# Attention layer of a two-layer tower: where the query and key products stand among the transposes

## The chip, the cores and the metric

The kernel is one program on 1 NeuronCore of a Trainium2 chip. The metric is the device time of one launch in microseconds (us). TensorE (PE) does matmuls and transposes, VectorE (DVE) and ScalarE (ACT) elementwise work, GpSimd (POOL) some more of it; SyncE (SP) issues DMAs. The engines run their own instruction streams in order and meet through semaphores.

## The reference, cut to what matters

16 sequences of 129 tokens (one class token, 128 others), 512 wide, pass four sublayers. Each one is h = h + f(layernorm(h)). The third, the one of this case, is gated linear attention:

```
x = layernorm(h)                      # per token, over 512
q = silu(x @ Wq.T) * SCALE            # Wq, Wk: 32 x 512
k = sigmoid(x @ Wk.T)
g = log_sigmoid(-k)
S_t = exp(g_t) * S_{t-1} + k_t v_t^T  # v = x, state 32 x 512
o_t = q_t S_t
go = o @ Wog.T + x @ Wig.T
f = rms_norm(o) * g_weight * go * sigmoid(go)
```

A mixture-of-experts layer stands before it and another behind it.

## The kernel before, in words

Tokens lie in 17 tiles: tile 16 (`NB`) has the 16 class tokens, and tiles 0 to 15 have 128 tokens of one sequence each. `ORDER` takes tile 16 first, so position i = 0 is the class tile and position i is tile i - 1 for i = 1 to 16. The norm is solved in four groups (`GROUPS`): the class tile, positions 1 to 4, positions 5 to 10, and positions 11 to 16. For each group VectorE takes statistics (L482), aggregates them (L506), solves the inverse root by small dependent instructions (L516 to L522) and writes the normed tiles into `xn` one by one (L527).

**TensorE** (`tensor` of `gla_layer`) waits for each tile of `xn` and turns it by four 128 x 128 transposes (`turn_tile`, L538) into one of three PSUM banks (`TB1`), so turn i also waits until ScalarE has copied out turn i - 3 (`tev`). A *quarter* q is four tiles, positions 4q + 1 to 4q + 4. `project(q)` (L2001) multiplies the four turned tiles of a quarter, 512 tokens, by the 64 query and key columns, in 4 fp32 matmuls that the profile records as 8. It waits for the copies of all turns up to position 4q + 4, writes into its own bank (`QK_BANKS[q]`) and raises `qk`. `project(-1)` does the 16 class tokens. Before the change the projections 0, 1 and 2 stand behind the turns at positions 6, 10 and 14, and projection 3 behind all.

**ScalarE** (`scalar`) copies each turn out into `xg` (L1920; two quarters fit, so a copy of quarter 2 or 3 waits for projection 0 or 1). `band_cls` (L1926, L1927) handles the class tokens. `band_of(q)` waits for projection q and writes queries (L1932, a copy) and keys (L1933, a sigmoid) of that quarter into 32 partitions. Before the change `band_of(0)`, `(1)` and `(2)` stand behind the copies at positions 7, 11 and 15, and `band_of(3)` behind all. Then two sigmoids over all quarters follow (L1948, L1949), and the copies of a second pass of turns (L1955).

**Behind it** TensorE goes through the tiles a second time: it turns each again, multiplies by the split gate weights (`rows_by`, L2029), does the attention products (L2054, L2061) and the outputs (L2080 to L2087). VectorE runs the decay scan and scales the keys (L1784 to L1805) once the sigmoids are there. SyncE waits for all five projections (`qk` at 5) before it loads the next layer's first shared weights.

Of the kernel before, what the change touches and what calls it, by code (L numbers as in the profile page):

```python
# [533 lines left out]
def turn_tile(t_eng, ps_bank, xn, t, ident):  # L534

    r = tile_rows(t)
    for k in range(KD):
        ins = t_eng.transpose(ps_bank[:, k * r:(k + 1) * r], xn[0:r, t, k * P:(k + 1) * P], ident[0:r, 0:r])  # L538
    return ins
# [1142 lines left out]
def gla_layer(nc, sem, sb, ps, d, hd, h_in, h_got, g, before, stored, xr_next, rest):  # L1682
# [7 lines left out]
    KH, BL, NBL, NG = 32, 32, 4, 4  # L1690
# [214 lines left out]
    def scalar(s):  # L1905
        s.wait_ge(w_in, 5 * 16)
        for w, to in ((wog, wo), (wig, wi)):
            s.activation(to[:, 0], w, ACT.Copy).then_inc(wsp, 1)

        def turn(i):  # L1910
            n = ORDER[i]
            r, q = rows_of(n), n // NG
            s.wait_ge(turned, i + 1)
            src = ps[:, TB1[i % 3], 0:KD * r].rearrange("p (k n) -> p k n", k=KD)
            if n == NB:
                s.activation(xg16, src, ACT.Copy).then_inc(tev, 1)
                return
            if q >= 2:
                s.wait_ge(qk, q)
            s.activation(xg[:, q % 2, :, (n % NG) * P:(n % NG + 1) * P], src, ACT.Copy).then_inc(tev, 1)  # L1920

        def band_cls():
            s.wait_ge(qk, 1)
            for q, band in enumerate(bands):
                cols = slice(NG * q, NG * q + NG)
                s.activation(qr[band, :, 0], ps[0:KH, CLS_BANK, cols], ACT.Copy).then_inc(bnd, 1)  # L1926
                s.activation(kk[band, :, 0], ps[KH:2 * KH, CLS_BANK, cols], ACT.Sigmoid).then_inc(bnd, 1)  # L1927

        def band_of(q):
            s.wait_ge(qk, q + 2)  # L1930
            src = ps[:, QK_BANKS[q], :].rearrange("p (b n) -> p b n", b=NG)
            s.activation(qr[bands[q], :, 1:SEQ], src[0:KH], ACT.Copy).then_inc(bnd, 1)  # L1932
            s.activation(kk[bands[q], :, 1:SEQ], src[KH:2 * KH], ACT.Sigmoid).then_inc(bnd, 1)  # L1933

        for i in range(T):
            turn(i)
            if i == 3:
                band_cls()
                for to in (xc3[0:NB], xc3[2 * KH:ROWS3]):
                    if to is not None:  # L1940
                        s.wait_ge(c3, 2)
                        s.activation(to, xn[0:NB, NB, :], ACT.Copy).then_inc(c3, 1)
            if i % 4 == 3 and i > 4:
                band_of((i - 7) // 4)
        for q in range(NG - 1, NG):
            band_of(q)
        s.wait_ge(bnd, 4 * NG)
        s.activation(sq, qr, ACT.Sigmoid).then_inc(bnd, 1)  # L1948
        s.activation(av, kk, ACT.Sigmoid, scale=-1.0).then_inc(bnd, 1)  # L1949

        def high_part(j):
            n = ORDER[j]
            r = rows_of(n)
            s.wait_ge(turned, T + j + 1)
            s.activation(xT[:, j % 2, 0, :, 0:r], ps[:, TB2[j % 2], 0:KD * r].rearrange("p (k n) -> p k n", k=KD), ACT.Copy).then_inc(tev, 1)  # L1955

        def xw_out(j):
            n = ORDER[j]
            r = rows_of(n)
            s.wait_ge(xwp, j + 1)  # L1960
            if j == 0:
                s.activation(xwc3[0:NB], ps[0:NB, XW_BANK, :], ACT.Copy).then_inc(c3, 1)
                s.activation(xwc3[2 * KH:ROWS3], ps[0:NB, XW_BANK, :], ACT.Copy).then_inc(c3, 1)
            s.activation(xw[0:r, j % 2], ps[0:r, XW_BANK, :], ACT.Copy).then_inc(xwr, 1)

        def square(j):
            r, u = rows_of(ORDER[j]), j % 2
            s.wait_ge(ob, j + 1)
            if j:
                s.wait_ge(ssr, j)  # L1970
            s.activation(junk[0:r], ps[0:r, O_BANKS[u], :], ACT.Square, accum_out=ss[0:r, j:j + 1]).then_inc(ssr, 1)

        def gate(j):
            r, u = rows_of(ORDER[j]), j % 2
            s.wait_ge(gor, j + 1)
            if j >= 2:
                s.wait_ge(pr, j - 1)
            s.activation(sg[0:r, u], ps[0:r, G_BANKS[u], :], ACT.Sigmoid).then_inc(sgr, 1)

        high_part(0)  # L1980
        high_part(1)
        xw_out(0)
        xw_out(1)
        s.wait_ge(acp, 1)
        s.activation(accF[0:ROWS3], ps[0:ROWS3, ACC_BANK, :], ACT.Copy).then_inc(atcr, 1)
        for j in range(T):
            if j >= 1 and j + 1 < T:
                high_part(j + 1)
            if 1 <= j and j + 1 < T:
                xw_out(j + 1)  # L1990
            square(j)
            gate(j)

    def tensor(t):
        t.wait_ge(w_in, 5 * 16)

        def project(q):
            w, bank = (NB, CLS_BANK) if q < 0 else (QC, QK_BANKS[q])
            t.wait_ge(tev, 1 if q < 0 else 4 * q + 5)
            for k in range(KD):  # L2000
                mm = t.matmul(ps[0:2 * KH, bank, 0:w], wqk[:, k, :], xg16[:, k, :] if q < 0 else xg[:, q % 2, k, :], start=(k == 0), stop=(k == KD - 1))  # L2001
            mm.then_inc(qk, 1)

        for i, n in enumerate(ORDER):
            t.wait_ge(xr, i + 1)
            if i >= 3:
                t.wait_ge(tev, i - 2)
            turn_tile(t, ps[:, TB1[i % 3], :], xn, n, ident).then_inc(turned, 1)
            if i == 3:
                project(-1)  # L2010
            if i % 4 == 2 and i > 4:
                project((i - 6) // 4)
        project(NG - 1)

        PARTS = ((0, 0), (0, 1), (1, 0))

# [81 lines left out]
        for j in range(T):  # L2098
# [8 lines left out]
            outs(j)  # L2107

    return sync, vector, gpsimd, scalar, tensor, qk


# [204 lines left out]
```

## Time and profile before

| | us |
|---|---|
| median of 3 runs | 1591.97 |
| lowest and highest | 1591.94, 1593.3 |
| the profiled execution, its time | 1593.97 |
| the profiled execution, its span | 1592.2 |
| TensorE busy with matmuls | 1389.7 |
| VectorE busy | 833.2 |
| ScalarE busy | 373.7 |
| mean granted clock of TensorE | 0.964 |

The span runs from the first instruction to the last. Busy time of an engine is a sum over stages with different limits, so it doesn't say what a change in one stage is worth. The granted clock is 1.0 at 2.4 GHz and 0.5 at 1.2 GHz, and a stretch with both shows a value between. The stage of this change lies between 661 and 707 us of the span.

### The profile page before, as it was taken

The numbers are of one execution on the slowest core, as the hardware profiler recorded it, in microseconds if no ns is written. First come the engines' busy times: TensorE is split into PE (matmuls) and PEld (weight loads), VectorE is DVE, ScalarE is ACT, GpSimd is POOL, SyncE is SP. The second block draws the span as 40 slices with busy tenths as digits, with TensorE's granted clock in tenths as the row PEclk, the third lists the DMA queues.
The fourth block names the chain that finished last, engine by engine and source line by source line (L and its number), as shares of the span: only waits on it lengthen the run. The fifth ranks groups of instructions, "written<-read, shape, count | busy, mean of one in ns | idle before, by whom it ended". The sixth has DMA issues, their size and how long they took to land.

```text
span 1592.2 us, 20911 instructions
## 1 busy us (share of the span) xinstructions
PE 1389.7 (87%) x6461; PEld 1077.6 (68%) x6462; DVE 833.2 (52%) x1711; ACT 373.7 (23%) x711; POOL 480.7 (30%) x350
## 2 busy tenths in 40 slices
PE   0585739999899999289999899999999979989996
PEld 0583317888444444137776688888888869879885
DVE  8875597655222222563667765555555533323332
ACT  1113114221111111232222312332333212212221
POOL 0662430351244443001211035433332111333441
PEclk9999779999999999689999999999999999999998
DMA  4492005102955554600000404666666588666553
GB/s 97 92 162 32 0 21 179 61 21 68 344 95 94 93 94 66 196 21 0 1 0 1 140 21 133 219 214 219 207 214 207 215 312 276 178 181 179 92 86 40
DMA packets 87387, 193.95 MB, mean 122 GB/s; under 512 B 28657, under 2 KB 32753, under 8 KB 83825
## 3 DMA queue, kind: packets, MB, share of 16 engines
q1 hardware_dynamic: 67232, 151.18, 29.4%
q0 software_dynamic: 20096, 42.02, 14.7%
q8 instruction: 33, 0.54, 0.1%
q14 instruction: 26, 0.21, 0.0%
HBM read 112.24 MB, written 77.87 MB: 119 GB/s over the span
## 4 chain that ended last, share of the span: by engine, by line
PE 62%; DMA 20%; DVE 11%; issue 4%; ACT 1%; POOL 0%; SPq 0%; POOLq 0%; DVEq 0%; ACTq 0%
PE ps L1507 22%; PE ps L1567 19%; DMA h_rows<-moe_scratch 7%; DMA h_rows<-held,moe_scratch 6%; PE ps L2029 6%; PE ps L429 4%; DMA out<-held,moe_scratch 3%; DVE held L482 2%; DMA out<-moe_scratch 2%; PE ps L538 1%; PE ps L2001 1%; PE ps L778 1%; PE ps L779 1%; PE ps L2054 1%; PE ps L1601 1%
## 5 line engine op out<-in xcount | busy, mean ns | idle before, releaser
L1567 PE MATMUL ps<-moe_rounded 128*128 128x384 f32 (+2 forms) x1800 | 374.1, 350 | 0.0
L1567 PEld LDWEIGHTS ps<-moe_rounded 128*128 128x128 f32 x1800 | 325.7, 188 | 32.9
L1277 DVE SCALAR_TENSOR_TENSOR held<-ps,moe_scratch,held 128x512 f32<-128x512 f32 (+1 forms) x255 | 187.4, 747 | 179.1 <-PE ps L1507 178.9
L1507 PE MATMUL ps<-moe_expert_parts,moe_rows_parts 128*128 (+1 forms) x1320 | 258.3, 348 | 4.7 <-DVE moe_rows_parts L1285 3.2
L1507 PE MATMUL ps<-moe_rounded 128*128 128x512 f32 (+3 forms) x885 | 239.2, 390 | 7.7 <-DVE moe_rounded L1259 5.7
L1507 PEld LDWEIGHTS ps<-moe_expert_parts,moe_rows_parts 128*128 128x128 f32 (+1 forms) x1320 | 218.7, 189 | 18.1 <-issue 5.4
L1507 PEld LDWEIGHTS ps<-moe_rounded 128*128 128x128 f32 (+2 forms) x885 | 145.4, 170 | 45.8 <-DVE moe_rounded L1259 8.1
L1291 DVE TENSOR_TENSOR moe_scratch<-moe_scratch,ps 128x256 f32<-128x256 f32 (+1 forms) x80 | 37.7, 471 | 230.2 <-ACT moe_scratch L1488 230.2
L1628 PE MATMUL ps<-moe_experts,moe_scratch 128*128 x320 | 145.9, 599 | 1.7 <-ACT moe_scratch L1474 1.1
L1383 POOL TENSOR_TENSOR moe_split_parts<-moe_scratch,moe_split_parts 128x704 fp32r<-128x704 f32 (+2 forms) x48 | 88.7, 1854 | 172.7 <-ACT moe_split_parts L1463 172.6
L1367 POOL DMA_INDIRECT slot_tokens<-moe_scratch x68 | 73.6, 1082 | 168.5 <-DVE held L1277 161.5
L1488 ACT ACTIVATE moe_scratch<-ps 128x256 f32<-128x256 f32 (+1 forms) x80 | 34.0, 425 | 326.8 <-PE ps L1628 191.5
L1450 ACT ACTIVATE moe_scratch<-ps 128x384 f32<-128x384 f32 (+2 forms) x75 | 38.7, 516 | 305.1 <-PE ps L1567 305.1
L429 PE MATMUL ps<-sb 128*128 128x64 f32 x256 | 56.5, 422 | 58.5 <-DVE sb L363 58.2
L2029 PE MATMUL ps<-gla_rounded 128*128 128x512 f32 (+1 forms) x408 | 100.8, 404 | 2.1 <-ACT gla_rounded L1955 2.1
L1628 PEld LDWEIGHTS ps<-moe_experts,moe_scratch 128*128 128x128 f32 x320 | 58.2, 192 | 60.7 <-issue 60.7
L429 PEld LDWEIGHTS ps<-sb 128*128 128x128 f32 x256 | 55.2, 332 | 59.3 <-POOL sb L384 57.9
L538 PE MATMUL ps<-held,moe_xn 128*128 128x128 f32 (+1 forms) x272 | 42.8, 306 | 59.5 <-DVE moe_xn L527 52.6
L2029 PEld LDWEIGHTS ps<-gla_rounded 128*128 128x128 f32 (+1 forms) x408 | 74.7, 186 | 22.4 <-issue 2.9
L538 PEld LDWEIGHTS ps<-held,moe_xn 128*128 128x128 f32 (+1 forms) x272 | 36.0, 160 | 74.5 <-DVE moe_xn L527 36.6
L1903 POOL TENSOR_TENSOR moe_xn<-moe_scratch 128x512 f32<-128x512 f32 (+1 forms) x17 | 25.6, 1506 | 199.2 <-DVE moe_scratch L1837 199.2
L1654 PE MATMUL ps<-moe_experts,moe_scratch 128*128 x160 | 75.4, 593 | 1.1 <-DVE moe_scratch L1313 1.1
(305 smaller groups left out, 1679.2 us busy)
## 6 DMA issues: line engine op xcount, KB each, us to landing
moe_expert_parts<-expert_parts SPq DMA_DIRECT2D x8, 3840.0 KB, 14.7
expert_parts<-moe_split_parts SPq DMA_DIRECT2D x32, 704.0 KB, 3.7
moe_scratch<-in_ffn_gate_up SPq DMA_DIRECT2D x32, 352.0 KB, 5.0
xn_rows<-moe_xn SPq DMA_DIRECT2D x2, 4096.0 KB, 12.8
moe_experts<-in_ffn_gate_up SPq DMA_DIRECT2D x8, 1024.0 KB, 12.6
expert_parts<-moe_split_parts SPq DMA_DIRECT2D x8, 1024.0 KB, 4.7
moe_scratch<-in_ffn_sh_gate_up SPq DMA_DIRECT2D x15, 512.0 KB, 3.5
tokens<-sb SPq DMA_DIRECT2D x16, 256.0 KB, 4.5
```

The source lines that it names most:

```text
L429: mm = t.matmul(o, ub[:, u, hh, :], bb[:, u, hh, :], start=True, stop=True)
L538: ins = t_eng.transpose(ps_bank[:, k * r:(k + 1) * r], xn[0:r, t, k * P:(k + 1) * P], ident[0:r, 0:r])
L1277: v.scalar_tensor_tensor(out=hb[0:rows, t, :], in0=ps[0:rows, ADDED[t % 3], :], scalar=sg[0:rows, t:t + 1], in1=hb[0:rows, t, :], op0=ALU. ...
L1291: v.tensor_tensor(ehid[:, u], esil[:, u], e_up(u), ALU.mult).then_inc(ehr, 1)
L1367: p.indirect_dma_start(out=slots, out_offset=bass.IndirectOffsetOnAxis(ap=pos_u[0:r, j, t:t + 1], axis=0), in_=tab_u[0:r, t, j, :], in_off ...
L1383: p.tensor_tensor(part[0:rows, x, 1, 0:w], raw[0:rows, x, 0:w], part[0:rows, x, 0, 0:w], ALU.subtract).then_inc(plr, 1)
L1450: s.activation(unit_sil(u, m), unit_banks(u, m)[0], ACT.Silu).then_inc(silr, 1)
L1507: mm = t.matmul(out, lhs(k, x), rhs(k, y), start=(k == 0 and i == 0), stop=(k == ks - 1 and i == 2))
L1567: mm = t.matmul(unit_banks(u, m)[j], weights(k, x, j), xT[y][:, k, unit_cols(m)], start=(k == 0 and i == 0), stop=(k == KD - 1 and i == 2))
L1628: mm = t.matmul(ps[:, u, 0:2 * F], xgT[:, u, k], exg(e, k, 0, 2 * F), start=(k == 0), stop=(k == KD - 1))
L1654: mm = t.matmul(ps[:, 6 + u, :], ehT[0:FR[f], u, f, :], exd(e, f, FR[f]), start=(f == 0), stop=(f == NF - 1))
L2029: mm = t.matmul(out[0:r], xT[:, j % 2, x, k, 0:r], w[:, y, k, :], start=(k == 0 and i == 0), stop=(stop and k == KD - 1 and i == 2))
```

## The change

Projection 0 moves from behind turn 6 to behind turn 4, which is the last turn of its norm group. Projection 1 stays behind turn 10, also the last of its group. Projection 2 moves from behind turn 14 to behind turn 16, right ahead of projection 3. On ScalarE `band_of(0)` moves from behind copy 7 to behind copy 8, `band_of(1)` from behind copy 11 to behind copy 12, and `band_of(2)` from behind copy 15 to behind copy 16, ahead of `band_of(3)`. No instruction is added or removed; the waits inside the moved functions move with them.

```diff
@@ ScalarE @@
-            if i % 4 == 3 and i > 4:
-                band_of((i - 7) // 4)
-        for q in range(NG - 1, NG):
+            if i == 8:
+                band_of(0)
+            if i == 12:
+                band_of(1)
+        for q in range(2, NG):
             band_of(q)
@@ TensorE @@
             if i == 3:
                 project(-1)
-            if i % 4 == 2 and i > 4:
-                project((i - 6) // 4)
-        project(NG - 1)
+            if i == 4:
+                project(0)
+            if i == 10:
+                project(1)
+        for q in range(2, NG):
+            project(q)
```

## Rows read from the trace of the kernel before

**Rows 1.** The page: span, then the chain that ended last, by engine and line.
```profile
span 1592.2 us, 20911 instructions
...
PE 62%; DMA 20%; DVE 11%; issue 4%; ACT 1%; POOL 0%; SPq 0%; POOLq 0%; DVEq 0%; ACTq 0%
```
**Rows 2.** Waits from 675 to 707: waiter, releaser, us in total, times, longest.
```profile
DVE gla_rounded L1774 <- ACT gla_rounded L1955: 14.1, 1, 14.1
...
ACT sb L1932 <- PE ps L2001: 5.4, 1, 5.4
...
PE ps L2001 <- ACT moe_scratch L1920: 4.2, 3, 2.1
```
**Rows 3.** Timeline of TensorE: start, length, what; in brackets idle before it, releaser.
```profile
670.86 1.12 PE L538 MATMUL ps<-held,moe_xn 128*128 128x128 f32 x4
675.63 1.97 PE L538 MATMUL ps<-held,moe_xn 128*128 128x128 f32 x8 [3.65 <-DVE moe_xn L527]
677.53 4.54 PE L2001 MATMUL ps<-moe_scratch,gla_raw 128*64 128x512 f32 x8
681.99 2.07 PE L538 MATMUL ps<-held,moe_xn 128*128 128x128 f32 x16
685.04 3.65 PE L2001 MATMUL ps<-moe_scratch,gla_raw 128*64 128x512 f32 x8 [0.98 <-ACT moe_scratch L1920]
688.62 2.07 PE L538 MATMUL ps<-held,moe_xn 128*128 128x128 f32 x16
691.81 3.65 PE L2001 MATMUL ps<-moe_scratch,gla_raw 128*64 128x512 f32 x8 [1.12 <-ACT moe_scratch L1920]
695.39 1.09 PE L538 MATMUL ps<-held,moe_xn 128*128 128x128 f32 x8
698.58 5.34 PE L2001 MATMUL ps<-moe_scratch,gla_raw 128*64 128x512 f32 x8 [2.09 <-ACT moe_scratch L1920]
...
706.94 9.42 PE L2029 MATMUL ps<-gla_rounded 128*16 128x512 f32 x33 [2.09 <-ACT gla_rounded L1955]
```
**Rows 4.** Timeline of ScalarE, the same columns.
```profile
675.09 0.60 ACT L1920 ACTIVATE moe_scratch<-ps 128x512 f32<-128x512 f32 x1
...
683.18 0.57 ACT L1932 ACTIVATE sb<-ps 32x512 f32<-32x512 f32 x1
683.78 0.59 ACT L1933 ACTIVATE sb<-ps 32x512 f32<-32x512 f32 x1
684.39 1.57 ACT L1920 ACTIVATE moe_scratch<-ps 128x512 f32<-128x512 f32 x3
...
696.71 0.58 ACT L1932 ACTIVATE sb<-ps 32x512 f32<-32x512 f32 x1
697.31 0.59 ACT L1933 ACTIVATE sb<-ps 32x512 f32<-32x512 f32 x1
697.92 0.60 ACT L1920 ACTIVATE moe_scratch<-ps 128x512 f32<-128x512 f32 x1
703.96 0.58 ACT L1932 ACTIVATE sb<-ps 32x512 f32<-32x512 f32 x1 [5.43 <-PE ps L2001]
```
**Rows 5.** Timeline of VectorE: the normed tiles of the last two groups, the same columns.
```profile
675.03 2.83 DVE L527 TENSOR_SCALAR moe_xn<-held 128x512 f32<-128x512 f32 x6
...
684.43 2.83 DVE L527 TENSOR_SCALAR moe_xn<-held 128x512 f32<-128x512 f32 x6
```
**Rows 6.** Stretches: length, busy of PE, PEld, DVE, ACT, POOL; granted clock, DMA share, GB/s.
```profile
675.70:679.60 3.90, 3.90 (x11) 2.19 (x12) 3.90 (x9) 1.20 (x2) 0.00 (x0) 0.53 0.01 2
...
683.50:700.10 16.60, 12.40 (x49) 5.49 (x49) 8.76 (x14) 8.13 (x15) 0.00 (x0) 0.99 0.01 1
700.20:703.50 3.30, 3.30 (x5) 0.69 (x4) 0.00 (x0) 0.00 (x0) 0.00 (x0) 0.54 0.00 0
703.60:706.90 3.30, 1.25 (x9) 0.74 (x8) 0.28 (x2) 2.87 (x6) 0.00 (x0) 0.96 0.59 184
...
724.10:730.80 6.70, 6.51 (x22) 5.23 (x21) 3.06 (x6) 0.89 (x2) 1.27 (x1) 0.52 0.00 0
730.90:870.60 139.70, 139.70 (x631) 104.86 (x630) 84.57 (x224) 37.42 (x80) 23.06 (x15) 1.00 0.00 1
```

## The prediction

> **What bounds the kernel now.** I read the page first. The span is 1592.2 us, and 62% of the chain that ended last is TensorE [rows 1]; the reader should see that the kernel has no spare engine to blame, but also that this says nothing of one stage. So next I read the waits of the stage in which the projections stand. TensorE's projections wait for ScalarE's copies of the turns, L1920, 3 times and 4.2 us in total; ScalarE waits 5.4 us for the last projection; and VectorE stands for 14.1 us until ScalarE's first copy of the second pass [rows 2]. That last wait is the important one: VectorE is not a competitor here, it idles until this stage is over, so whatever TensorE and ScalarE save here, it starts sooner.
>
> The timeline of TensorE shows where the 4.2 us lie: 0.98 ahead of projection 1, 1.12 ahead of projection 2, and 2.09 ahead of projection 3 [rows 3]. The timeline of ScalarE says why. Ahead of projection 3 the engine did not only copy turns 15 and 16: between them it did `band_of(2)`, 696.71 to 697.9, and only at 697.92 the copy of turn 16 that projection 3 waits for [rows 4]. In the same way `band_of(0)`, 683.18 to 684.37, stood ahead of the copy of turn 8, and projection 1 started at 685.04 right behind it [rows 3, 4]. VectorE had its part ready: the last six tiles were written from 684.43 to 687.26 [rows 5], while TensorE turned the first of them only at 688.62 [rows 3]. From turn 11 on the norm is no bound.
>
> Last I read the granted clock by stretches. It is at the lower level (1.2 GHz) until nearly 679.6, at the upper (2.4 GHz) from there to 700.1, at the lower from 700.2 to 703.5, and at the upper after it [rows 6]. The fall at 700 came 1.5 us into projection 3, after the 2.09 us gap. It shows in the duration: 5.34 us for the same 8 records that took 3.65 twice [rows 3]. So that gap cost 2.09 us as idle time and 5.34 - 3.65 = 1.69 us as a slow projection.
>
> **The change part by part.** No instruction comes or goes, so the sum is a new schedule of the same pieces. Prices at the upper clock: a projection 3.58 us from its start to the start of what follows (685.04 to 688.62), a turn 2.07 / 4 = 0.52 us, both [rows 3]; a copy 0.60 us alone and 1.57 / 3 = 0.52 us in a row, a band (both instructions) 684.39 - 683.18 = 1.21 us, both [rows 4].
>
> *Projection 0 behind turn 4.* It waits for copy 4, which runs from 675.09 to 675.69 [rows 4]. ScalarE can't make it sooner, since `band_cls` and two copies of the class tile stand ahead. Turns 5 and 6 are queued behind this wait and would have started at 675.63 [rows 3], when their first normed tile was written [rows 5]. So the added wait costs 0.1 us, and the 3.65 us in which TensorE stood idle before 675.63 are not filled: I give this "fill" nothing. If copy 4 came earlier by some other edit it would be worth up to that 3.65. Projection 0 now runs at the lower clock until 679.65: in those 3.95 us it gets half of that done, 1.98 of its 3.65, and ends at 681.3. The low stretch is spent either way, on two turns and half a projection before, on a projection after.
>
> *Turns 5 to 10 in a row.* 681.3 + 6 x 0.52 = 684.4. The three banks allow it: a turn needs the copy of three turns before, and copies at 0.52 to 0.60 us each keep up with turns at 0.52 with `band_of(0)` out of the way. It stands behind copy 8 now, at about 684.0. Projection 1 needs copy 8, ready at 684.0, so it starts at 684.4 without the wait of 0.98, and the next turns start at 688.0 instead of 688.62. Here the gain is only 0.6 us: 0.98 less what the later start of the turns at the low clock and the added wait took.
>
> *Turns 11 to 16 in a row.* Start 688.0. Copies 11 and 12 end at 689.1 and 689.7, `band_of(1)` runs to 690.9, copy 13 to 691.5. Turn 16 reuses the bank of turn 13 and waits for that copy, where it would have started at 690.6: a new stall of 0.9 us. Its bounds are 0 and 1.2, a whole band. The turns end at 692.0.
>
> *Projections 2 and 3 back to back.* Projection 2 runs 692.0 to 695.6. It covers copies 14 to 16, done by 693.1, so the waits of 1.12 and 2.09 both go. Projection 3 follows at once and ends at 699.2, if the clock holds. `band_of(2)` runs beside projection 3, 1.21 us under 3.6 us; without that cover it would come back on the path at its 1.21. Behind projection 3 all is as before: `band_of(3)` at once (0.03 us behind it in rows 4), two sigmoids, first copy of the second pass, and the next matmul 706.94 - 703.92 = 3.0 us behind the end of projection 3 [rows 3].
>
> *The sum.* Projection 3 ended at 703.92 and ends at 699.2: 4.7 us less. By kinds: waits of 4.2 go, 0.9 comes, 0.1 and about 0.2 of copies that trail are lost: 3.0 us of order; and 1.7 us of clock. Behind it nothing swallows the gain: TensorE is busy for all 139.7 us from 730.9 to 870.6 [rows 6], VectorE's 14.1 us wait only gets shorter with it, and SyncE's loads for the next layer wait for the same projections, so they move along. The profiled execution took 1593.97, so 1589.3. That execution was 2.0 us above the median of the runs, 1591.97, and the forecast goes by the median: 1587.3.
>
> *What I can only bound.* The clock's falls further on (0.52 over the 6.7 us from 724.1 [rows 6]) come at moments that I can't place for a program shifted by 4.7 us. One such fall is worth 1.7 us, by the 1.69 above. I take none, with 1.7 up and down as its bounds.
>
> **The rivals.** *The clock gives nothing.* Either the timed runs did not have the fall at 700 (the profiled execution is 2.0 us slower than the median, which is the size of one fall), or a new fall replaces it, because the stretch from 688 to 692 holds turns and a stall of 0.9 and no projection. Then only the order counts: 3.0 us, 1589.0. For it: the fall came where the gap was longest. Against: turns and a gap of 1.12 between projections 1 and 2 did not bring it down (0.99 from 683.5 to 700.1 [rows 6]). The Trainium skill, "TensorE: Matmul & The Clock Gate", section "Part 4: PE-mode transpose", says that transposes do not count as busy in the way matmuls do for the full clock. By that rule six turns in a row are a poor stretch, projection 2 would run at the lower level, and the time would be this rival's; this trace has turns only mixed with projections, so it neither bears it out nor refutes it.
>
> *The clock gives twice.* The stretch of small class products ahead of 724 moves too, and the 6.7 us low stretch becomes one of half the length: 1.7 us more, 1585.6.
>
> *No change.* ScalarE is the bound of the tail, so removing the order's waits only moves them to `band_of(3)`. Against it: ScalarE waited 5.4 us for the last projection [rows 2]. 1592.0.
>
> *Slower.* The projections use 64 of the 128 columns. If projection 0, alone at the front, does not raise the clock as the mix of two turns and a projection did at 679.6, the whole piece up to the end of projection 3 runs at the lower level. From 679.65 on it holds 18.6 us of TensorE work, which becomes 37.2; the 0.9 stall vanishes in it: 17.7 more, less the gain of 4.7, so 1605. Each us of low clock costs half a us of progress, so it decides from 9.4 us of additional low stretch on. Against it: from 700.2 to 703.5 nothing but projection 3 ran, at 0.54, and the clock was back up (0.96) in the stretch behind [rows 6].
>
> **How the numbers follow.** Forecast 0.55; clock gives nothing 0.25; clock gives twice 0.12; no change 0.05; slower 0.03. The forecast's own range is 1586.3 to 1588.5: the new stall between 0 and 1.2. The range with the clock's cases, and 1.7 either way behind the stage, is 1585.0 to 1590.2. Within 0.2%, 3.2 us, is about what a measurement of this kernel can't tell from no change; the border is 1588.8. Of the second case some two thirds lie inside it, all of the fourth and a little of the first: 0.24. Slower 0.03, faster 0.73.
>
> **What would show it.** Right: in the changed profile's TensorE timeline six turns stand in a row twice, the wait of L2001 for L1920 is under 0.3 us in total, turn 16 waits about 0.9, and the two last projections take 7.2 us together. Projection 0 starts between 675.6 and 675.8 relative to the same start of the norms. The 14.1 us wait of VectorE shrinks to about 9.4. Wrong: a projection of over 4 us behind 690, or a stretch of clock 0.5 between 690 and 700, says that the clock's share failed; a wait of turns 8 to 10 for copies says that ScalarE can't keep up; an equal end of the last projection with a gain elsewhere says that I named the wrong cause.

## The result, and the profile after

| | before | changed |
|---|---|---|
| median us (runs) | 1592.46 (14) | 1589.32 (14) |
| lowest to highest | 1588.72 to 1595.16 | 1587.16 to 1592.84 |
| profiled span | 1592.2 | 1588.1 |

The ratio of the times is 0.9981, 95% interval 0.9973 to 0.9989: 3.0 us less, 1.8 to 4.3. Run once more, beside new runs of the kernel before, the changed kernel gave 0.9973 (0.9962 to 0.9983). The forecast of 1587.3 is 2.0 us too low. The stated range of 1585.0 to 1590.2 held the time, and the direction was right. Half a us of the 2.0 is the kernel before: its median over 14 runs is 1592.46, and the forecast stood on 1591.97 from three.

TensorE's timeline of the changed kernel, which answers to [rows 3] (start, length, what; in brackets the idle time and what ended it):

```profile
669.96 0.66 PE L538 MATMUL ps<-held,moe_xn 128*128 128x128 f32 x4
674.83 6.02 PE L2003 MATMUL ps<-moe_scratch,gla_raw 128*64 128x512 f32 x8 [4.22 <-ACT moe_scratch L1920]
680.78 3.04 PE L538 MATMUL ps<-held,moe_xn 128*128 128x128 f32 x24
683.75 3.65 PE L2003 MATMUL ps<-moe_scratch,gla_raw 128*64 128x512 f32 x8
687.33 2.55 PE L538 MATMUL ps<-held,moe_xn 128*128 128x128 f32 x20
691.10 0.63 PE L538 MATMUL ps<-held,moe_xn 128*128 128x128 f32 x4 [1.22 <-ACT moe_scratch L1920]
691.66 7.08 PE L2003 MATMUL ps<-moe_scratch,gla_raw 128*64 128x512 f32 x16
...
701.76 5.72 PE L2034 MATMUL ps<-gla_rounded 128*16 128x512 f32 x24 [2.09 <-ACT gla_rounded L1957]
```

The three waits of 0.98, 1.12 and 2.09 us are gone. Two are left: 4.22 ahead of projection 0, in the place of the 3.65 ahead of turn 5, and a new one of 1.22 ahead of turn 16 (691.10). The two last projections run as one piece of 7.08 us. ScalarE shows what turn 16 waited for (to be held against [rows 4]):

```profile
688.02 1.09 ACT L1920 ACTIVATE moe_scratch<-ps 128x512 f32<-128x512 f32 x2 [2.32 <-PE ps L538]
689.13 0.59 ACT L1932 ACTIVATE sb<-ps 32x512 f32<-32x512 f32 x1
689.75 0.59 ACT L1933 ACTIVATE sb<-ps 32x512 f32<-32x512 f32 x1
690.36 2.06 ACT L1920 ACTIVATE moe_scratch<-ps 128x512 f32<-128x512 f32 x4
```

Band 1 stands between copies 12 and 13, and turn 16 needs the bank that copy 13 empties. The waits of the same stretch, answering to [rows 2]:

```profile
DVE gla_rounded L1774 <- ACT gla_rounded L1957: 9.4, 1, 9.4
...
PE ps L2003 <- ACT moe_scratch L1920: 4.2, 1, 4.2
...
PE ps L538 <- ACT moe_scratch L1920: 1.2, 1, 1.2
```

VectorE's wait fell from 14.1 to 9.4, as forecast. The first of the two PE waits is the one ahead of projection 0. The stretches (columns as in [rows 6]):

```profile
666.60:669.90 3.30, 3.26 (x20) 2.94 (x20) 3.30 (x7) 1.60 (x3) 0.00 (x0) 0.58 0.78 236
670.10:673.30 3.20, 0.52 (x4) 0.28 (x3) 2.94 (x15) 3.00 (x10) 0.00 (x0) 0.92 0.01 2
673.50:680.10 6.60, 5.27 (x7) 1.57 (x8) 6.41 (x16) 1.23 (x3) 0.00 (x0) 0.53 0.00 1
680.30:700.90 20.60, 18.16 (x82) 8.96 (x80) 11.15 (x29) 11.74 (x22) 0.00 (x0) 1.00 0.06 19
```

No fall between 680 and 701. Here the clock rose once already at 669.4 and fell again in the idle time ahead of projection 0.

I measure the **stage** from the start of the four-tile statistics (L482, 661.22 before, 660.72 after) to the end of projection 3. It was 703.92 - 661.22 = 42.7 us and is 698.74 - 660.72 = 38.0: 4.7 less between these two traces. The span lost 4.1. The rest adds up like this: 0.5 comes from ahead of the stage; behind it 1.2 is gained up to the last turns of the second pass (two pieces of low clock before, one after); and 2.2 are lost from there to the end, where the changed kernel's trace has low stretches at 926 and at 1284, of which this trace of before has none. The change touches no instruction there. The one at 1284 is in three other traces of the kernel before too. The one at 926 is in both traces of the changed kernel and in none of the four of the kernel before, whose clock is 1.00 from 925 to 935. It costs about half its 3.3 us, 1.6 us (an estimate: the clock was at half). So the shifted program may well lose again behind the stage a part of what it gained in it. Why it falls there is not shown: TensorE's wait just ahead is 1.77 us long in the changed kernel and 1.74 in the kernel before. The stretch in the two traces of the changed kernel, and then in the kernel before:

```profile
926.00:929.30 3.30, 3.30 (x11) 2.81 (x11) 0.95 (x2) 0.50 (x1) 1.92 (x2) 0.57 0.02 6
```

```profile
926.70:930.20 3.50, 3.50 (x11) 3.10 (x11) 1.17 (x2) 0.49 (x1) 1.67 (x2) 0.53 0.16 59
```

```profile
926.00:935.00 9.00, 7.26 (x37) 6.35 (x36) 6.76 (x10) 1.37 (x3) 1.78 (x2) 1.00 0.27 88
```

### The profile page after: what moved, and what is told of

It reads as the page before. It is cut to its first block, busy times and chain, and to the rows that moved or that the text cites. A ratio compares the mean times of both kernels' runs of the same rounds, so it can differ in the third digit from the quotient of the medians.

```text
span 1588.1 us, 20911 instructions
## 1 busy us (share of the span) xinstructions
PE 1388.7 (87%) x6461; PEld 1078.0 (68%) x6462; DVE 833.4 (52%) x1711; ACT 373.0 (23%) x711; POOL 480.2 (30%) x350
## 3 DMA queue, kind: packets, MB, share of 16 engines
q0 software_dynamic: 20096, 42.02, 14.6%
## 4 chain that ended last, share of the span: by engine, by line
PE 61%; DMA 21%; DVE 11%; issue 4%; ACT 2%; POOL 0%; SPq 0%; POOLq 0%; DVEq 0%; ACTq 0%
PE ps L1507 21%; PE ps L1567 19%; DMA h_rows<-moe_scratch 7%; DMA h_rows<-held,moe_scratch 6%; PE ps L2034 6%; PE ps L429 4%; DMA out<-moe_scratch 3%; DMA out<-held,moe_scratch 3%; PE ps L538 2%; DVE held L482 1%; PE ps L778 1%; PE ps L2003 1%; PE ps L779 1%; PE ps L2059 1%; PE ps L1601 1%
## 5 line engine op out<-in xcount | busy, mean ns | idle before, releaser
L1450 ACT ACTIVATE moe_scratch<-ps 128x384 f32<-128x384 f32 (+2 forms) x75 | 38.7, 515 | 306.9 <-PE ps L1567 301.5
```

What stands on the lines that cost most here:

```text
L1450: s.activation(unit_sil(u, m), unit_banks(u, m)[0], ACT.Silu).then_inc(silr, 1)
```

## The experiments

All edits are to the kernel named in each; "idle" is TensorE's idle time in the stage between turn 4 and the end of projection 3. Ratios are to runs of the kernel before on the same chip. Stages and idle times are from one trace each, where no number is given; in the two kernels with fills a fill counts as busy. Two traces of one kernel may differ in the stage by the clock. Their idle times agree better, but the clock enters there too: where turn 4 runs at the upper clock (0.66 us) and not at the lower (1.12), TensorE arrives sooner and stands up to 0.7 us longer ahead of the next piece. It did so in both traces of the changed kernel and in two of the kernel before.

| kernel | idle us | stage us | ratio (95%) | less than before, us |
|---|---|---|---|---|
| before, 4 traces | 7.8 to 8.5 | 41.2 to 42.7 | 1 | |
| changed, 2 traces | 5.4, 5.4 | 38.0, 38.6 | 0.9981 (0.9973 to 0.9989); again 0.9973 (0.9962 to 0.9983) | 3.0; 4.3 |
| act_only | 4.4 | 38.7 | 0.9960 (0.9947 to 0.9973) | 6.4 |
| pe_only | 7.9 | 40.7 | 0.9992 (0.9981 to 1.0003) | 1.3 |
| late_bands | 3.8 | 36.5 | 0.9971 (0.9961 to 0.9981) | 4.6 |
| cls_late | 2.8 | 35.2 | 0.9956 (0.9944 to 0.9969) | 7.0 |
| both | 0.7 | 34.4 | 0.9944 (0.9931 to 0.9957) | 8.9 |
| scalar_best | 4.4 | 38.4 | 0.9977 (0.9965 to 0.9989) | 3.7 |
| after_warm | 3.6 | 36.1 | 0.9970 (0.9956 to 0.9984) | 4.8 |
| before_filled | 6.0 | 41.3 | 0.9994 (0.9986 to 1.0003) | 1.0 |

**1. ScalarE's order alone** (act_only). The kernel before, with the ScalarE half of the diff.

> Only ScalarE's order is changed (bands 0, 1, 2 behind copies 8, 12, 16); TensorE's order is that of before. Stage length, from the start of the four-tile statistics (L482) to the end of projection 3, was 42.7 us before and 38.0 after the change. Theory A (the band ahead of an awaited copy was the cost; TensorE's order is worth nothing): projection 1 at once behind turn 10, projection 2 behind turn 14, a wait of 0.7 ahead of projection 3, stage 37.5 us, so 0.5 us better than the full change; time 3 to 5 us under before. Theory B (what counts is that projections 2 and 3 stand together behind all turns): stage 41 us or more and under 1.5 us of gain.

TensorE's timeline of this run, from projection 1 on:

```profile
684.21 3.65 PE L2003 MATMUL ps<-moe_scratch,gla_raw 128*64 128x512 f32 x8
687.79 2.06 PE L538 MATMUL ps<-held,moe_xn 128*128 128x128 f32 x16
689.79 3.65 PE L2003 MATMUL ps<-moe_scratch,gla_raw 128*64 128x512 f32 x8
693.36 1.09 PE L538 MATMUL ps<-held,moe_xn 128*128 128x128 f32 x8
695.20 3.65 PE L2003 MATMUL ps<-moe_scratch,gla_raw 128*64 128x512 f32 x8 [0.74 <-ACT moe_scratch L1920]
```

Of the waits only 0.74 us is left, as expected, and that with the projections still behind turns 10 and 14. The stage is 38.7 and not 37.5, since projection 0 took 5.78 us here and 4.54 in the trace from which I had worked it out: the same 8 records, more of them at the low clock. So by the stage it is not the 0.5 us better than the whole change that I expected; the time is 6.4 us less, more than the 3 to 5 expected, with 4.3 inside its interval. Theory B fell: putting projections 2 and 3 together is not what gains.

**2. TensorE's order alone** (pe_only). The kernel before, with the TensorE half of the diff.

> Only TensorE's order is changed; ScalarE's bands stay behind copies 7, 11 and 15. Theory A: band 2 now waits for projection 2 and stands ahead of copy 16, so projection 3 starts about 1.8 us behind projection 2; stage 40.7 us (42.4 if the clock falls in projection 3), 2.0 us of gain or 0.3. Theory B: stage 38 to 39 us, nearly the whole gain of the change.

The timelines of this run, TensorE's and then ScalarE's:

```profile
683.81 3.65 PE L2001 MATMUL ps<-moe_scratch,gla_raw 128*64 128x512 f32 x8 [0.97 <-ACT moe_scratch L1920]
...
690.67 1.11 PE L538 MATMUL ps<-held,moe_xn 128*128 128x128 f32 x8 [1.22 <-ACT moe_scratch L1920]
691.71 3.65 PE L2001 MATMUL ps<-moe_scratch,gla_raw 128*64 128x512 f32 x8
697.27 3.65 PE L2001 MATMUL ps<-moe_scratch,gla_raw 128*64 128x512 f32 x8 [1.91 <-ACT moe_scratch L1920]
```

```profile
695.40 0.58 ACT L1932 ACTIVATE sb<-ps 32x512 f32<-32x512 f32 x1 [3.41 <-PE ps L2001]
696.01 0.59 ACT L1933 ACTIVATE sb<-ps 32x512 f32<-32x512 f32 x1
696.62 0.60 ACT L1920 ACTIVATE moe_scratch<-ps 128x512 f32<-128x512 f32 x1
```

Stage 40.7 as worked out, and idle time of 7.9, the same as before: the waits moved and their sum stayed. The time can't be told from before. The stage is 0.4 us under the shortest of the four traces of before, so a small gain isn't excluded. ScalarE stood 3.41 us for projection 2 with copy 16 queued behind its band.

**3. Bands where they delay no copy** (late_bands).

```diff
-            if i == 8:
+            if i == 10:
                 band_of(0)
-            if i == 12:
+            if i == T - 1:
                 band_of(1)
```

> The changed kernel with band 0 behind copy 10 and band 1 behind copy 16, so that no band stands ahead of a copy that a turn waits for. Theory A: the stall of turn 16 (1.2 us in the changed kernel's trace) goes, stage 37.0 us against 38.0; 1 us less than the changed kernel. Rival (bands only move, ScalarE's sum is the bound of the tail): band 1 and band 2 delay band 3 and the stage's sigmoids, no gain.

TensorE's timeline from turn 11 on, and ScalarE's `band_of(3)`:

```profile
687.67 3.04 PE L538 MATMUL ps<-held,moe_xn 128*128 128x128 f32 x24
690.65 7.08 PE L2003 MATMUL ps<-moe_scratch,gla_raw 128*64 128x512 f32 x16
```

```profile
697.76 0.58 ACT L1932 ACTIVATE sb<-ps 32x512 f32<-32x512 f32 x1 [2.24 <-PE ps L2003]
```

Six turns in a row without a stall; stage 36.5. Against the changed kernel's 38.0 that is 1.5 less: 1.35 by the stall of turn 16, and 0.55 by the clock in projection 0 (5.47 against 6.02 us), which started 0.4 later. Bands 1 and 2 ran beside the projections and delayed nothing: band 3 found ScalarE idle for 2.24 us and started right behind projection 3, so the rival fell by the trace. The ratios, 4.6 us less against 3.0 and 4.3, overlap in their intervals and show no gain over the changed kernel.

**4. The idle time ahead of projection 0** (cls_late).

```diff
-            if i == 3:
+            if i == 4:
                 band_cls()
```

> The changed kernel with the class bands and the class copies behind copy 4 instead of copy 3, so that projection 0 can start at about 10 us from the start of the four-tile statistics instead of 14. Theory A (TensorE's 4.2 us of idle time ahead of projection 0 are only an order of ScalarE, and the path runs through projection 0): stage 34.6 us, 3.4 less than the changed kernel, and 6 to 8 us under before. Rival (the path runs through VectorE's last group of normed tiles, so an earlier projection 0 only waits for turn 11 instead): the gain stops at 0.6 to 1.5 us.

TensorE's timeline, from projection 0 on:

```profile
673.72 5.00 PE L2003 MATMUL ps<-moe_scratch,gla_raw 128*64 128x512 f32 x8 [0.69 <-ACT moe_scratch L1920]
...
686.11 2.55 PE L538 MATMUL ps<-held,moe_xn 128*128 128x128 f32 x20 [0.83 <-DVE moe_xn L527]
689.88 0.63 PE L538 MATMUL ps<-held,moe_xn 128*128 128x128 f32 x4 [1.23 <-ACT moe_scratch L1920]
```

Projection 0 starts 11.4 us into the stage instead of 14.1. The stage is 2.8 shorter than the changed kernel's (3.4 expected), and the time is 7.0 us less than before. Behind turn 4 VectorE now holds TensorE up for the first time, with 0.83 ahead of turn 11. The rival's bound of 0.6 to 1.5 was passed, so VectorE was not what bounded the changed kernel, but it is the next bound.

**5. Both of these** (both).

> The changed kernel with both of ScalarE's edits: class bands and copies behind copy 4, band 0 behind copy 10, band 1 behind copy 16. Theory A (each wait of TensorE for a copy is an order of ScalarE and they add): the stall of turn 16 (1.23 us in the run with the class copies late) goes and the idle time ahead of projection 0 stays at 0.7; what is left is 0.8 to 2.7 us of waiting for VectorE ahead of turn 11. Stage 34.0 us (35.24 with the class copies late alone, 36.52 with late bands alone), total 7 to 9 us under before. Rival (VectorE's last group sets the end, so the two don't add): stage 35 us, no better than the class copies late alone.

TensorE's timeline, from projection 0 to the end of projection 3, and VectorE's last six normed tiles:

```profile
672.55 6.40 PE L2003 MATMUL ps<-moe_scratch,gla_raw 128*64 128x512 f32 x8 [0.69 <-ACT moe_scratch L1920]
678.88 3.04 PE L538 MATMUL ps<-held,moe_xn 128*128 128x128 f32 x24
...
685.43 3.04 PE L538 MATMUL ps<-held,moe_xn 128*128 128x128 f32 x24
688.40 7.08 PE L2003 MATMUL ps<-moe_scratch,gla_raw 128*64 128x512 f32 x16
```

```profile
684.32 2.83 DVE L527 TENSOR_SCALAR moe_xn<-held 128x512 f32<-128x512 f32 x6
```

From 672.55 to 695.48 TensorE has no gap. The expected wait of 0.8 to 2.7 us ahead of turn 11 did not come, and that is luck of the clock: projection 0 took 6.40 us here and 5.00 in cls_late, so turn 11 came later than its tile, the first of the six from 684.32 on. Stage 34.4 (34.0 expected), median 1583.79 against 1592.29: the lowest time of this study, 8.9 us less than before (6.8 to 11.0). Its interval overlaps that of cls_late (4.9 to 8.9); that the two edits add is shown by the waits, not by the times.

**6. ScalarE's best order without TensorE's** (scalar_best). The kernel before with the class bands behind copy 4 and bands 0, 1, 2 behind copies 10, 14, 16.

> TensorE's order of before with all of ScalarE's edits: class bands and copies behind copy 4, band 0 behind copy 10, band 1 behind copy 14, band 2 behind copy 16. Theory A' (TensorE's early projection 0 is worth the idle time ahead of turn 5, but only once copy 4 is early): here TensorE still stands for 3.7 us ahead of turn 5, stage 37.4 to 38.7 us, 3 to 4 us longer than with both orders (34.37). Rival (TensorE's order is worth nothing, as ScalarE's order alone suggested): stage 34 to 35 us.

TensorE's timeline, turns 5 and 6, projection 0, and then projection 3:

```profile
675.74 1.97 PE L538 MATMUL ps<-held,moe_xn 128*128 128x128 f32 x8 [3.65 <-DVE moe_xn L527]
677.64 5.49 PE L2005 MATMUL ps<-moe_scratch,gla_raw 128*64 128x512 f32 x8
...
696.04 3.65 PE L2005 MATMUL ps<-moe_scratch,gla_raw 128*64 128x512 f32 x8 [0.74 <-ACT moe_scratch L1920]
```

Stage 38.4, 4.0 longer than with both orders, and the 3.65 us ahead of turn 5 stand as before. So TensorE's order shows no gain in the change as made, and is worth about 4 us of the stage once copy 4 is early: some 3.0 by the early projection 0 (3.65 us idle against 0.69), and 0.74 by the wait ahead of projection 3, which is gone where projection 2 stands there. The rival fell.

**7. What the low clock costs** (after_warm). The changed kernel; the added results are never read.

```diff
+        def fill(n):
+            for _ in range(n):
+                t.matmul(ps[0:2 * KH, QK_BANKS[3], :], wqk[:, 0, :], wog[:, 0, :], start=True, stop=True)
...
+            if i == 0:
+                fill(3)
...
             if i == 4:
+                fill(2)
                 project(0)
```

> The changed kernel with five 512-column matmuls whose result is never read, put into TensorE's idle times: three behind the class turn, two behind turn 4. Clock theory (the low clock from the start of the stage until about 680 costs what it lasts, since projection 0 is on the path): the clock is up before projection 0, which takes 3.65 us instead of 6.02, and the stage is 36.0 us against 38.0; time about 2 us under the changed kernel. Rival (projection 0 is not on the path, or low clock there is hidden by VectorE): stage stays at 38, time equal or up by the delay of turn 1.

The stretches of this kernel, then its projection 0:

```profile
662.30:667.50 5.20, 5.20 (x7) 1.14 (x6) 4.72 (x21) 0.22 (x1) 0.00 (x0) 0.50 1.05 388
667.60:670.00 2.40, 2.40 (x25) 2.20 (x24) 2.40 (x6) 1.74 (x5) 0.00 (x0) 1.00 0.82 255
670.20:674.40 4.20, 1.90 (x5) 0.43 (x4) 3.89 (x18) 3.97 (x11) 0.00 (x0) 1.00 0.09 22
```

```profile
674.46 5.29 PE L2003 MATMUL ps<-moe_scratch,gla_raw 128*64 128x512 f32 x8 [2.36 <-ACT moe_scratch L1920]
```

The stage came to 36.1, as expected, but only in part by the expected way. With the fill the clock was up from 667.6 on, yet it fell again at the start of projection 0, behind an idle piece of 2.36 us; projection 0 took 5.29, not 3.65. The other part is that faster turns let copy 4 and so projection 0 start earlier: 12.9 us into the stage instead of 14.1, 1.2 of the 1.9 us gained. In the time nothing of it can be seen: 1589.29 against 1588.37 for the changed kernel on the same chip.

**8. The fall ahead of projection 3** (before_filled). The kernel before, with `fill(2)` of experiment 7 ahead of `project(NG - 1)`.

> The kernel before with two 512-column matmuls whose result is never read ahead of the wait of projection 3, in the idle time of 2.09 us. Clock theory (the gap of 2.09 brings the clock down in projection 3, here and in a good part of the timed runs): projection 3 takes 3.65 us instead of 5.34, stage 41.0 instead of 42.7, time 0.8 to 1.7 us under before. Rival (the fall was chance of that execution, not tied to the gap): same time as before within 0.5 us. If the two matmuls don't fit they cost up to 0.3 us.

TensorE's timeline, the fill and projection 3:

```profile
697.58 1.93 PE L2006 MATMUL ps<-gla_raw 128*64 128x512 f32 x4
699.74 3.65 PE L2001 MATMUL ps<-moe_scratch,gla_raw 128*64 128x512 f32 x8 [0.23 <-ACT moe_scratch L1920]
```

Projection 3 took 3.65 us. The time is 0.9994 (0.9986 to 1.0003): it can't be told from before, and doesn't say how often there is a fall to prevent.

**9. Three more traces of the kernel before** (before_look1 to 3), unchanged.

> The kernel before once more, for its trace. If the fall of the clock in projection 3 belongs to the gap of 2.09 us, projection 3 takes 5.3 us here too; if it depends on how the chip's looks fall on the program, it takes 3.65 in some of the three traces and the forecast's term of 1.7 us was one execution's. Idle times 3.7, 1.0, 1.1 and 2.1 us in each.

> The same as for the first look at the kernel before: projection 3 of 5.3 us in all three by the first theory, of 3.65 in some by the second; stage 42.7 or 41.0 us accordingly.

> The same as for the first look at the kernel before. With the first trace that makes four: a share of about one half slow would put the clock's term of the forecast at 0.9 us on average instead of 1.7.

Projection 3 in each of the three:

```profile
697.02 3.65 PE L2001 MATMUL ps<-moe_scratch,gla_raw 128*64 128x512 f32 x8 [2.09 <-ACT moe_scratch L1920]
```

```profile
698.12 3.65 PE L2001 MATMUL ps<-moe_scratch,gla_raw 128*64 128x512 f32 x8 [2.09 <-ACT moe_scratch L1920]
```

```profile
699.48 3.65 PE L2001 MATMUL ps<-moe_scratch,gla_raw 128*64 128x512 f32 x8 [2.09 <-ACT moe_scratch L1920]
```

The wait is 2.09 us in all three. The slow projection is in none. The 5.34 us on which the forecast's clock term rests belong to one of four executions looked at. The idle time ahead of turn 5 was 4.32, 3.65 and 4.16 us, and not 3.7 in each: in the first and the third the clock was up for turn 4.

**Also run**: the changed kernel again (after_again).

> The changed kernel once more, for comparison on the same chip and for a second trace. Order theory: idle time of TensorE inside the stage 5.4 us again (4.2 and 1.2) and gain over before of 3 us. If the clock's share is real but not constant, the length of projection 0 or of the pieces behind differs from the first trace by up to 1.7 us while the idle times stay equal.

Its idle times are 4.21 and 1.22, its projection 0 took 6.23 us, its stage 38.6.

## Why the prediction came out 2 us low

**The waits: right.** That each wait for a copy was an order of ScalarE's, that the three would go, that VectorE would only wait less (9.4, the number forecast) and that the last projections take 7.2 together (7.08): all borne out. The clock-free part was forecast at 3.0 us, and 4.2 us of waits went for the one of 1.22. That the time fell by 3.0 as well is partly luck, since it also holds what the clock gave and took. The idle time fell by 7.84 - 5.44 = 2.4 in the first pair of traces, mostly because of the clock in turn 4 (below). One sign of being right was badly put: the wait of L2001 for L1920 was to be under 0.3 us, but it is 4.2, the wait ahead of projection 0. The forecast's own schedule has that wait, with projection 0 behind copy 4.

**The new stall of turn 16: right in place, small in size.** 1.22 instead of 0.9, the upper bound named. With late bands it is gone from the trace.

**The added wait of turns 5 and 6: right.** The idle time ahead went from 3.65 to 4.22, but the clock had been up for turn 4 (0.66 instead of 1.12), so TensorE arrived earlier and not the work later. Projection 0 started 14.11 us into the stage in the first trace and 14.45 in the second, against turn 5's 14.41 before. So no more than the 0.1 us forecast was lost; the sign named for it, 675.6 to 675.8 or 14.4 to 14.6 into the stage, fits the second trace and is missed by 0.3 in the first.

**The clock's 1.7 us: the term that was too large.** The forecast said that the gap "cost 2.09 us as idle time and 5.34 - 3.65 = 1.69 us as a slow projection". The idle time is the kernel's, the slow projection was that execution's: three other traces have the same gap and projections of 3.65. The average stage of the four traces of before is (42.7 + 41.6 + 41.2 + 41.8) / 4 = 41.8, that of the two of the changed kernel 38.3. The difference is 3.5: the 3.0 of order, and about a quarter of 1.69. With the stage of one trace, 42.7, I got 4.7. So the rival that came nearest is "the clock gives nothing", in its first form, with 1589.0; I gave it 0.25 although its evidence stood in the text: that execution was 2.0 us over the median, about the size of a fall.

**The clock behind the stage: taken as nothing, and not settled.** The low stretch of 6.7 us at 724 became one of 3.2 at 721 in the first trace (0.58), which is what "the clock gives twice" said. From the end of projection 3 to the end of the second pass the four traces of before took 163.6 to 166.1 us and the two of the changed kernel 163.6 and 163.7. From there to the end they took 721.3 to 723.5, and 723.3 and 725.7. On average 1.5 us came and 2.2 went, the latter with the low stretch at 926. Six traces that differ by up to 2.5 us can't price this, but the two pieces nearly cancel, and the time shows 3.0 to 4.3 us.

**The range was put too high at its upper end.** With 0.9 us of stall in the forecast and bounds of 0 and 1.2, the forecast's own range is 1586.4 to 1587.6, and not 1586.3 to 1588.5; with 1.7 either way it is 1584.7 to 1589.3. The measured 1589.32 lies at the end of that, so that the stated range held it owes something to this slip.

**What takes part in the change.** The prediction treated both engines' edits as one schedule. Taken apart, ScalarE's alone has less idle time (4.4) than the whole (5.4), 0.5 of it by the clock in turn 4, and TensorE's alone gains nothing that shows. The prediction saw that an earlier copy 4 would be worth "up to that 3.65" and left it there. Together with TensorE's order it took 2.8 us off the stage (38.0 to 35.2) and, with late bands, 2.1 (36.5 to 34.4), of the 7.4 between the average before and the best version.

**Open.** Whether ScalarE's order alone is faster than the changed kernel: 6.4 us less (4.3 to 8.4) against 3.0 and 4.3 in the two runs of the changed kernel, but the closely related scalar_best, with the same idle time, gave 3.7 (1.8 to 5.6). The traces differ by 1.0 us of idle time, or 0.5 without the clock in turn 4, less than these intervals; the stage of act_only is 38.7 against 38.0 and 38.6.

## What to carry to other kernels

When an engine waits for a small copy of its neighbour, look at what that neighbour did just ahead of it: work that nobody waits for yet belongs behind the copies that free a bank or complete an operand, into the time when the neighbour would stand anyway. A reordering of two engines should be taken apart, because one half can show no gain alone and be worth several us once the other is right. And a term that rests on the clock in one trace must be weighed by how often it comes: compare that execution with the median before the term goes into the sum.

## What the runs showed of the clock

The clock rose between 669.3 and 669.5 in the changed kernel, although TensorE had been idle for 5.32 us up to 666.64 and then ran nothing but twelve 128 x 128 transposes until the class projection began at 669.39:

```profile
669.10:669.30 0.20, 0.20 (x2) 0.00 (x0) 0.20 (x2) 0.14 (x1) 0.00 (x0) 0.50 0.54 119
669.30:669.50 0.20, 0.20 (x3) 0.11 (x3) 0.20 (x1) 0.01 (x1) 0.00 (x0) 0.75 0.74 201
669.50:669.70 0.20, 0.20 (x5) 0.20 (x6) 0.20 (x2) 0.20 (x1) 0.00 (x0) 1.00 0.66 177
```

With late bands six turns in a row stood twice between full projections without a fall. So the rule of the Trainium skill's page "TensorE: Matmul & The Clock Gate", section "Part 4: PE-mode transpose", which the forecast weighed and which the page states beside a time for bf16, does not hold for these fp32 transposes: the clock can come up on them alone. It doesn't always: in the first trace of the kernel before the same twelve ran and the clock stayed at 0.50 up to 675.6. Under that rule projection 2 would have run at the lower level behind six turns; it ran at the upper in every trace here.

Gaps of the same length had different outcomes: 2.09 us ahead of projection 3 brought a fall once in four traces, 2.36 us ahead of projection 0 did in after_warm, and 1.91 us in pe_only did not; 1.77 us ahead of 924 brought one in the changed kernel, and 1.74 ahead of 930 none in the kernel before. Projection 0, the same 8 records, took 4.54 to 6.40 us over all traces. The stage of the kernel before is 41.2 to 42.7 us long in its four traces, with waits that agree within 0.01 us apart from the one behind turn 4.
